# Conv, attention and expert layer in one kernel: no semaphore offset, start-up loads on two queues, constants in three parts

## The reference

```python
x = x + conv3x3(group_norm(x, 32 groups), L0_conv_weight)   # padding 1
t = x as tokens                                             # (8, 3136, 64)
t = t + attention(layer_norm(t), Wq, bq, Wk, bk, Wv, bv)    # one head, softmax over 3136 keys
n = layer_norm(t)
p = softmax(n @ gate_w + gate_b); the top 2 of 16 experts, weights divided by their sum
t = t + sum over the 2 experts of weight * ((silu(n @ w1) * (n @ w2)) @ w3)
x = t as images
```

## Time and profile before

| | us |
|---|---|
| median of 3 runs | 2741.71 |
| lowest and highest run | 2737.01, 2741.85 |
| span of the profiled execution | 2736.8 |
| TensorE busy | 2503.4 (91% of the span) |
| VectorE busy | 1832.0 (67%) |
| ScalarE busy | 1316.8 (48%) |
| GpSimd busy | 1019.0 (37%) |

### The profile page before, as it was taken

One profiled execution on the slowest core, in us unless ns is written; L12 is line 12 of the kernel. 1 busy time (PEld: TensorE's weight loads), 2 busy tenths in 40 slices (PEclk: granted clock), 3 DMA queues, 4 the chain that ended last, 5 costly groups with the idle time before them and its releaser, 6 DMA issues.

```text
span 2736.8 us, 46413 instructions
## 1 busy us (share of the span) xinstructions
PE 2503.4 (91%) x13821; PEld 1603.6 (59%) x13821; DVE 1832.0 (67%) x5227; ACT 1316.8 (48%) x2985; POOL 1019.0 (37%) x1097
## 2 busy tenths in 40 slices
PE   4799999999999999999999999999999999997773
PEld 2455555566666666566666666566666666564662
DVE  3666677676766777676867777676867776764432
ACT  1244444455554555455555555455555555453542
POOL 2012104400344324442344334443344324465765
PEclk8899999999999999999999999999999999998876
DMA  2124211111122122122121212122121111122442
GB/s 61 39 64 90 50 28 40 48 37 39 48 55 61 47 57 62 54 53 55 55 61 52 57 46 70 55 54 52 53 60 51 44 47 53 54 50 64 120 95 53
DMA packets 226555, 152.94 MB, mean 56 GB/s; under 512 B 100240, under 2 KB 216720, under 8 KB 226320
## 3 DMA queue, kind: packets, MB, share of 16 engines
q1 hardware_dynamic: 192208, 98.97, 14.0%
q0 software_dynamic: 31456, 48.03, 7.1%
q10 hardware_dynamic: 2656, 2.98, 0.4%
HBM read 83.92 MB, written 65.27 MB: 55 GB/s over the span
## 4 chain that ended last, share of the span: by engine, by line
PE 62%; DVE 13%; issue 5%; DMA 2%; POOL 2%; SPq 1%; ACT 1%; POOLq 0%; DVEq 0%; ACTq 0%
PE ps_o L1466 16%; PE ps_s L1454 8%; PE ps_m L1426 8%; PE ps_s L1455 7%; PE ps_x L1625 4%; DVE max_part L1105 4%; PE ps_z L1639 3%; PE ps_z L1492 3%; PE ps_x L1632 2%; PE ps_z L1614 2%; PE ps_y L1529 1%; DMA tc<-kept 1%; PE ps_s L1625 1%; PE ps_y L1545 1%; POOL got L783 1%
## 5 line engine op out<-in xcount | busy, mean ns | idle before, releaser
L1105 DVE TENSOR_REDUCE max_part<-ps_m 128x1 f32<-128x448 f32 x1400 | 858.6, 621 | 517.1 <-PE ps_m L1426 497.0
L950 ACT ACTIVATE prob<-ps_s 128x448 f32<-128x448 f32 x1400 | 757.3, 543 | 527.0 <-PE ps_s L1455 502.9
L1466 PE MATMUL ps_o<-prob,v_s 128*64 128x448 f32 x2800 | 683.0, 562 | 0.0
L1454 PE MATMUL ps_s<-q_a,k_a 128*128 128x448 f32 x1400 | 593.5, 424 | 1.6 <-ACT q_a L942 0.7
L783 POOL DMA_INDIRECT got<-sorted_y,slot x448 | 428.3, 956 | 433.0 <-PE ps_s L1455 209.5
L762 POOL DMA_INDIRECT sorted_x<-xn,slot x448 | 429.8, 959 | 350.3 <-issue 154.7
L1426 PE MATMUL ps_m<-k_a,q_a 128*128 128x448 f32 (+3 forms) x1600 | 530.0, 358 | 28.2 <-DVE max_part L1105 22.4
L1455 PE MATMUL ps_s<-q_b,k_a 128*128 128x448 f32 x1400 | 511.9, 366 | 0.0
L1426 PEld LDWEIGHTS ps_m<-k_a,q_a 128*128 128x128 f32 (+1 forms) x1600 | 298.7, 188 | 92.7 <-DVE max_part L1105 61.5
L1454 PEld LDWEIGHTS ps_s<-q_a,k_a 128*128 128x128 f32 x1400 | 265.9, 190 | 142.3 <-ACT prob L950 106.5
L1466 PEld LDWEIGHTS ps_o<-prob,v_s 128*64 128x64 f32 x2800 | 153.5, 135 | 224.9 <-issue 161.1
(11 more groups left out here) (186 smaller groups left out, 3031.6 us busy)
## 6 DMA issues: line engine op xcount, KB each, us to landing
fx<-sorted_x SPq DMA_DIRECT2D x43, 384.0 KB
sorted_y<-fy SPq DMA_DIRECT2D x42, 320.0 KB
xh<-in_x SPq DMA_DIRECT2D x96, 126.0 KB, 2.7
fx<-sorted_x SPq DMA_DIRECT2D x47, 256.0 KB
sorted_x<-fy POOLq DMA_DIRECT2D x28, 320.0 KB, 6.0
sorted_x<-xn,slot POOLq DMA_INDIRECT x448
got<-sorted_y,slot POOLq DMA_INDIRECT x448
x_now<-in_x SPq DMA_DIRECT2D x112, 56.0 KB, 2.3
```

What stands on the lines that cost most here:

```text
L950: a.activation(prob[(at.n * KEY_TILES + i) % PROBS][:], ps_s[(at.n * KEY_TILES + i) % 2][:, 0:CHUNK], ACT.Exp).then_inc(s["p_ready"], 1)
L1105: v.tensor_reduce(max_part[n % 2][0:here.stop - here.start, j, kb:kb + 1], ps_m[(passes_before(n) + m) % 2][0:here.stop - here.start, 0:CH ...
L1454: t.matmul(ps_s[t_of % 2][:, 0:CHUNK], k_a[p][:, keys], high, start=True, stop=False)
L1466: t.matmul(ps_o[side:side + CHANNELS, 0:CHUNK], v_s[u % 2][:, i, :], prob[(n * KEY_TILES + i) % PROBS][:], start=(i < 2), stop=(i >= KEY_T ...
```

## The change

It has five parts, all of which act before the body begins.

1. The offset is gone. `started` and the 108 increments are removed, each wait counts from zero, and a wait for zero is left out (`wait_past`).
2. The image is loaded from two queues: SyncE issues the upper half of each chunk, ScalarE the lower half, then `raw_w` and the biases.
3. On SyncE the first chunk's rows come right after the image, `raw_a` after them.
4. GpSimd writes its constants in three parts. `consts` reaches 1 after the identity, `pair_mean`, `minus_half`, `xg` and small ones, 2 after those that the lead-in of image 0 reads, and 3 after the rest, which stands behind the first and second `norm1`.
5. ScalarE runs one activation of a constant before it needs one, so that its function table is loaded there. `gate_bb` and `gate_s` are issued behind it. VectorE and TensorE do the convolution weights ahead of the attention weights.

```diff
-    engine.wait_ge(sem, value)
-    engine.nop(nofuse=True)
+    if value > 0:
+        engine.wait_ge(sem, value)
+        engine.nop(nofuse=True)
...
         @block.sync
         def _(sp):
-            sp.wait_ge(started, 1)
             for c in range(CHUNKS):
-                for half in range(2):
-                    sp.dma_start(first_image[c][64 * half:64 * half + 64, :], x_v[0, :, half_of(c, half)])\
-                        .then_inc(s[f"image_in{c}"], 16)
-...
+                sp.dma_start(first_image[c][0:64, :], x_v[0, :, half_of(c, 0)]).then_inc(s[f"image_in{c}"], 16)
...
             load_halo(0, 0, 0)
+            for m, w in enumerate((wq, wk, wv)):
+                sp.dma_start(raw_a[:, m, :], w).then_inc(s["weights_in"], 16)
             load_halo(0, 1, 1)
             load_stats(LEADS[0])
-            sp.wait_ge(s["stats_done"], ONE + CHUNKS)
+            sp.wait_ge(s["stats_done"], CHUNKS)
...
         def _(pool):
-            for n in names:
-                if n not in ("zeroed", "scattered0", "scattered1", "gathered0", "gathered1"):
-                    g.sem_inc(s[n], 1)
-            g.sem_inc(started, 1)
-            pool.wait_ge(started, 1)
...
             group_rstd(0)
-            for at in LEADS:
+            norm1(LEADS[0])
+            more_constants()
+            norm1(LEADS[1])
+            last_constants()
+            for at in LEADS[2:]:
                 norm1(at)
+            wait_apart(pool, s["consts"], 3)
             group_rstd(1)
...
         def _(act):
-            act.wait_ge(started, 1)
...
+            for c in range(CHUNKS):
+                act.dma_start(first_image[c][64:128, :], x_v[0, :, half_of(c, 1)]).then_inc(s[f"image_in{c}"], 16)
+            for half in range(2):
+                act.dma_start(raw_w[64 * half:64 * half + 64, :], conv_w).then_inc(s["conv_w_in"], 16)
+            for to, bias in ((wq_a[:, 0, 0:1], bq), (wk_a[:, 1, 0:1], bk), (wv_a[:, 0, 0:1], bv), (wv_a[:, 1, 0:1], bv)):
+                act.dma_start(to, bias.rearrange("(c a) -> c a", a=1)).then_inc(s["weights_in"], 16)
+            act.wait_ge(s["consts"], 1)
+            a.activation(z_s[:, 0:128], ident[:], ACT.Copy)
+            act.dma_start(gate_bb[:], gate_b.rearrange("(a c) -> a c", a=1).partition_broadcast(TILE)
+                          .rearrange("p a c -> p (a c)")).then_inc(s["weights_in"], 16)
+            for half in range(2):
+                act.dma_start(gate_s[64 * half:64 * half + 64, :], gate_w).then_inc(s["weights_in"], 16)
+            wait_apart(act, s["consts"], 2)
             normed(LEADS[0])
```

More of the change, by code:

```diff
@@ L201, in __call__ @@
         self.count += 1
-        (wait_apart if apart else type(self.engine).wait_ge)(self.engine, self.sem, ONE + self.start + self.count)
+        (wait_apart if apart else type(self.engine).wait_ge)(self.engine, self.sem, self.start + self.count)
 class At:
@@ L540, in _ @@
         def _(sp):
-            sp.wait_ge(started, 1)
             for c in range(CHUNKS):
-                for half in range(2):
-                    sp.dma_start(first_image[c][64 * half:64 * half + 64, :], x_v[0, :, half_of(c, half)])\
-                        .then_inc(s[f"image_in{c}"], 16)
[L546 to L555, removed]
+                sp.dma_start(first_image[c][0:64, :], x_v[0, :, half_of(c, 0)]).then_inc(s[f"image_in{c}"], 16)
             def load_halo(b, c, count):
                 if count >= 2:
-                    wait_apart(sp, s["xconv_ready"], ONE + count - 1)
+                    wait_apart(sp, s["xconv_ready"], count - 1)
                 for half in range(2):
@@ L716, in _ @@
                 chain(g.tensor_copy(pair_mean[mine, other], pair_mean[mine, mine]))
[L718 to L720 removed]
             chain(g.memset(minus_half[:], -0.5))
[L722 to L733 removed]
+            chain(g.memset(xg[:], 0.0))
+            chain(g.memset(wq_a[:, 1, 0:1], 0.0))
+            chain(g.memset(wk_a[:, 0, 0:1], 0.0))
+            g.memset(gn_q[:], 0.0).then_inc(s["consts"], 1)
+            chain(g.memset(w_out[:], 0.0))
+            for half in range(2):
+                chain(g.memset(w_out[64 * half:64 * half + 1, CHANNELS:OCOLS], 1.0))
+            chain(g.memset(v_give[:, :, 0:1], 1.0))
+            chain(g.memset(xn[:, :, :, 0:1].bitcast(f32), 1.0))
+            for p in range(1):
                 chain(g.memset(v_s[p][96:128, :, :], 0.0))
@@ L736, in _, with more_constants, last_constants @@
                 chain(g.memset(key_tiles(p)[:, FILLED:KEY_TILES, TILE:128].bitcast(f32), 0.0))
-            chain(g.memset(v_give[:, :, 0:1], 1.0))
-            chain(g.memset(xn[:, :, :, 0:1].bitcast(f32), 1.0))
-            chain(g.memset(wq_a[:, 1, 0:1], 0.0))
-            chain(g.memset(wk_a[:, 0, 0:1], 0.0))
-            chain(g.memset(w_out[:], 0.0))
-            for half in range(2):
-                chain(g.memset(w_out[64 * half:64 * half + 1, CHANNELS:OCOLS], 1.0))
-            chain(g.memset(t_out[:, :, CHANNELS:128], 0.0))
-            chain(g.memset(fy[0][:], 0.0))
-            g.memset(gn_q[:], 0.0).then_inc(s["consts"], 1)
+            g.memset(ones[:], 1.0).then_inc(s["consts"], 1)
+            def more_constants():
+                wait_apart(pool, s["consts"], 2)
+                chain(g.affine_select(out=before[:], in_=ones[:], compare_op=ALU.is_gt, fill=0.0, base=0,
+                                      pattern=[[1, TILE]], channel_multiplier=-1))
+                for first, last in FX_PARTS:
+                    for j in range(2 * (last - first)):
+                        chain(g.memset(digit[:, 2 * first + j:2 * first + j + 1], float(EXPERTS ** j)))
+                chain(g.iota(expert_i[:], pattern=[[1, EXPERTS]], base=0, channel_multiplier=0))
+                chain(g.iota(tile_i[:], pattern=[[SLOTS, SORTED_TILES]], base=0, channel_multiplier=0))
+                chain(g.tensor_copy(expert_f[:], expert_i[:]))
+                chain(g.tensor_copy(tile_f[:], tile_i[:]))
+            def last_constants():
+                for many, starts in not_first.items():
+                    chain(g.memset(starts[:], 1.0))
+                    chain(g.memset(starts[:].rearrange("p (e t) -> p e t", t=many)[:, :, 0:1], 0.0))
+                chain(g.memset(v_s[1][96:128, :, :], 0.0))
+                chain(g.memset(v_s[1][0:TILE, :, 0:1], 1.0))
+                chain(g.memset(key_tiles(1)[:, FILLED:KEY_TILES, TILE:128].bitcast(f32), 0.0))
+                chain(g.memset(t_out[:, :, CHANNELS:128], 0.0))
+                g.memset(fy[0][:], 0.0).then_inc(s["consts"], 1)
             def zero(p, c):
@@ L986, in _ @@
             v = nc.vector
-            dve.wait_ge(started, 1)
             def last_of_image(event):
@@ L1403, in _ @@
             t = nc.tensor
-            pe.wait_ge(started, 1)
-            pe.wait_ge(s["consts"], ONE + 1)
+            pe.wait_ge(s["consts"], 1)
             def maxima(n, u, which):
```

302 lines of the change are left out of this document (146 added, 156 removed).

## The result

| | us |
|---|---|
| changed kernel, median of 5 runs | 2724.30 (2721.49 to 2725.67) |
| kernel before, median of 5 runs beside it | 2741.39 (2737.01 to 2741.85) |
| ratio, with its 95% interval | 0.9939 [0.9928, 0.9949] |
| profiled execution | 2721.7, its span 2720.0 |

What follows compares the result with a forecast made beforehand. The bound was the chain of short steps before the first convolution. Moving that from 33.46 to 16.75 saves 16.7 us, 8.7 from the increments and 8.0 from the rest: 2741.7 - 16.7 = 2725.0, range 2719 to 2731.

Steps and rivals of the forecast that it cites:

- Increments: Before any engine's first work: without the increments all engines go at 0.8 instead of 9.54, 8.7 us saved.
- late start of the engines: Rival at the kernel's start: something the increments hid holds the engines; 0 to 8.7 us lost, half gives 2729.4; chance 0.08.
- Image: Image loads at the start: two queues issue side by side, saving 4.45 us; aggregate begins at 7.5, ends at 7.8.
- taking turns: Rival at the image loads: the two queues alternate at generating descriptors; gain only 7.0 us, 2734.7; chance 0.16.
- Constants: GpSimd's start-up writes: first part ends at 5.3, covered by the statistics; the rest fits GpSimd's holes, at zero cost.
- Statistics to `xg`: Start-up chain from the aggregate to the normalized chunk: TensorE starts at 7.9, `scale` ends at 12.0, `xg` at 13.6.
- Weights last, behind the gate loads: End of the start-up: gate loads land at about 14.0, `wq_a` waits for them, first convolution at 16.75.
- Early table: ScalarE's start-up: function table, 1.28 us with the next activation right behind, is loaded by the time `xg` needs it.
- drain behind it: Rival on ScalarE at start-up: a 1380 ns drain after the table load costs 1.4 us, giving 2726.4; chance 0.05.
- Clock: Lead-in's seven convolutions: the shift may mix the clock anew, -8 to +5 us about the sum.
- low clock in the steady part: Rival from 127 to 2420 us: 40 us at low level eat the gain, 53 make it slower, 2747.2; chance 0.03.
- Reference point: Whole-kernel time: the 16.7 us gain is set against the median 2741.7, not the profiled execution 4.9 below it.

Runs made afterwards that it cites:

- the repeat: The changed kernel run again with no edit, to compare the other runs with; 2723.74 us.
- offset only: The kernel before with only the increments and start semaphore removed and waits for zero left out; 2733.75 us, ratio 0.998.
- weights in the gap: The changed kernel with gate loads on their own semaphore, `raw_a` issued earlier, and attention weights formed while GpSimd takes the power; 2722.06 us, ratio 0.9936.

## Why the prediction was right, and where not

- **Increments.** Predicted 8.7 us for all. (The 8.8 of the earlier trace rows is the length of SyncE's wait; the prediction words it as a distance behind the last increment, but its 8.7 is taken from the right moments, 0.8 and 9.54.) Measured 8.76 alone and 8.64 when doubled. The late start of the engines, a rival, is out: the first load is at 0.80.
- **Image.** Side by side was right, and taking turns is out. The aggregate came at 8.18, not 7.5. The term was 0.7 too small: SyncE's 7 pieces ended at 5.57 instead of 5.3, since they took 0.68 each beside the other queue, and the aggregate began 2.6 behind the end of issue instead of 2.17. In the repeat it was 7.90, so 0.3 of it differs between runs.
- **Constants.** The first part ended at 5.14 (predicted 5.3), before the aggregate, the second at 8.01, and the rest fitted in GpSimd's holes. The cost of zero was right; the split itself is worth 6.9 us.
- **Statistics to `xg`.** Predicted `gn_bias` by 12.0 and `xg` by 13.6; they were done at 12.52 and 14.14. Late by the 0.7 of the aggregate, less 0.2.
- **Weights last, behind the gate loads.** Here a step failed: "the last lands at about 14.0", and `wq_a` waits for it. The prediction took the instructions of ScalarE in order; the queue issued `gate_bb` 0.07 us after the table load began. `wq_a` started at 13.12, right behind `wT` (12.44 and 0.55), with no wait in its row. So VectorE's own order held it, not a load, though by little: without the early table `wq_a` waited 0.18 for `gate_s` at 13.01. The weights were last all the same: with them in the gap the start moved by 1.6. (The convolution's row names the memset of `xg`'s border, L1068, as its releaser; it stands on VectorE right behind `qk_lo`.) The sum was 0.8 too late (16.75, measured 15.95): 0.9 too much here, and 2.83 instead of 2.75 from there to the convolution.
- **Early table.** The prediction had the table out of the way when `xg` needs it, and so it was; but that is not the edit's doing, since without it the load finds room in the wait for `gn_bias`. The drain behind it, which the Trainium skill ("ScalarE: Activation LUTs", What ACT_TABLE_LOAD costs) puts at 1380 ns, doesn't show: the activation starts 1.29 us after the load does.
- **Clock.** Bounds -8 to +5; measured +1.0, for a granted clock of 0.73 instead of 0.74. Kernels with the same start differ by 2 there. Over all runs the lead-in took from 76.4 (offset only, 0.76) to 80.0 (weights in the gap, 0.71). The rival of a low clock in the steady part is out (1.00).
- **Reference point.** I set the gain against the median, not the profiled run. The start moved by 17.5, the lead-in took 1.0 more, the medians differ by 17.1. That the forecast of 16.7 is within 0.4 of it is partly luck, twice over. The start came 0.8 earlier than the sum had it, and the lead-in took 1.0 more, so two misses cancel. And the medians scatter: runs of one kernel lie 2.4 to 8.1 us apart, for the most part through a body that VectorE's wait for `tc` stretches, which no step of the prediction named; the two profiles compared here happen to have nearly the same body (2388.8 and 2388.4).

Removing the increments alone brought 5.8 in time for 9.9 at the first scores (111.00 to 101.06). The profiles place most of that: the span is 6.8 shorter, the body 4.0 longer, and what follows the last scores 0.9 shorter. The wait for `tc` was longer there, 55.3 us over 800 to 2420 against 48.7, which fits. Left open is why that wait differs from one execution to the next.

## What to carry to other kernels

Look at what all engines wait for before their first instruction: here 107 increments of a semaphore, 81 ns each, stood in front of everything, and removing them took 8.8 us off the start. After that a start-up is a race of several chains. Taken out alone, the other parts that were tested are worth 3.8 us (queues), 6.9 (constants) and nothing (table); together that is more than the 8.7 that the increments leave, since each counts only while its chain ends last, so put each part back alone to see which one does. And look for waits that recur: one load issued a turn ahead brought 12 to 13 us, some three quarters of what the whole start did, and made the steady part the same length in every profile, so that small gains elsewhere can be read.

## What the hardware showed that I had not expected

- Two queues issued loads at once with hardly a loss: 0.63 and 0.70 us for each piece, against 0.64 to 0.68 on one queue.
- ScalarE's queue issues DMAs while the engine loads its function table (9.27, within 9.20 to 10.48).
- A function table is loaded before the last semaphore of its activation has come: at 11.18, with `gn_bias` at 12.21.
- With the same work and a start within 15.80 to 15.95, five profiles had a mean granted clock of 0.72 to 0.74 over the lead-in and reached the first scores at 92.71 to 94.80. A gain of 1.6 us ahead of such a stretch can't be read behind it from one profile: it was gone in one kernel (94.31) and there in another (93.31 against 94.80).
